# A two-layer transformer on one core: the feed-forward's turns counted on VectorE alone, its queues reordered, the identity inside the output weights

## The reference

```python
o = s @ w_o
return s + o                                  # end of the third step, s: heads' outputs

hidden = x @ W1 + b1                          # 128 -> 512
imag = w_imag * sin(theta + hidden * 0.1)
quantum_phase = cos(theta) * w_real + sin(theta) * w_imag
q = hidden + quantum_phase * imag * 0.1
out = relu(q) @ W2 + b2                       # 512 -> 128
x = x + out
```

## Time and profile before

| | us |
|---|---|
| three executions | 1871.88, 1875.59, 1877.41 (median 1875.59) |
| the profiled execution, its own time | 1856.86 |
| its span, first to last instruction | 1855.0 |
| mean granted TensorE clock, share of full speed | 0.943 |
| busy in the span: PE, DVE, ACT, POOL | 1708.5 (92%), 1372.3 (74%), 1143.6 (62%), 308.6 (17%) |
| chain that ended last: PE, DVE, ACT, issue, POOL, DMA | 73%, 14%, 4%, 4%, 3%, 3% |
| last instruction of the second attention ends | 1738.85 |
| last finish ends (its store follows) | 1852.33 |

### The profile page before, as it was taken

The page is one execution under the profiler, slowest core; times in us unless marked ns, Lnnn a source line. Parts: engine busy times, 40 slices in busy tenths (PEclk is TensorE's granted clock), DMA queues, the critical chain, the costliest instruction groups (busy, mean ns, idle before and its releaser), DMA issues.

```text
span 1855.0 us, 30812 instructions
## 1 busy us (share of the span) xinstructions
PE 1708.5 (92%) x10574; PEld 723.3 (39%) x10574; DVE 1372.3 (74%) x2373; ACT 1143.6 (62%) x2396; POOL 308.6 (17%) x407
## 2 busy tenths in 40 slices
PE   6599999999999899998789999999999999999876
PEld 3244444444443366655312232232222222322455
DVE  7678888788887155464897888888888888882486
ACT  4156666756664543333406777777777777777776
POOL 5000000002231237363500000000000000000265
PEclk9589999999998899999658999999999999998998
DMA  9555454423400012222411111111111111000000
GB/s 258 137 118 127 131 141 118 49 31 56 58 22 14 26 35 71 68 67 60 119 33 14 18 18 18 18 18 18 18 18 18 18 18 18 1 2 1 1 23 24
DMA packets 97577, 93.73 MB, mean 51 GB/s; under 512 B 47214, under 2 KB 75507, under 8 KB 95376
## 3 DMA queue, kind: packets, MB, share of 16 engines
q1 hardware_dynamic: 87360, 53.70, 16.7%
q0 software_dynamic: 9920, 37.87, 5.8%
q10 hardware_dynamic: 144, 0.20, 0.1%
HBM read 48.03 MB, written 40.86 MB: 48 GB/s over the span
## 4 chain that ended last, share of the span: by engine, by line
PE 73%; DVE 14%; ACT 4%; issue 4%; POOL 3%; DMA 3%; SPq 0%; POOLq 0%; DVEq 0%; ACTq 0%
PE ps L877 20%; PE ps L861 18%; PE ps L828 17%; DVE rowmax L1513 7%; PE ps L1038 2%; PE ps L1058 2%; PE ps L1030 2%; PE ps L1048 2%; PE ps L893 2%; PE ps L831 1%; PE ps L864 1%; ACT probs L1251 1%; DMA V<-v 1%; PE ps L1015 1%; DVE K L1857 1%
## 5 line engine op out<-in xcount | busy, mean ns | idle before, releaser
L1513 DVE TENSOR_REDUCE rowmax<-ps 128x1 f32<-128x1024 f32 (+7 forms) x1024 | 977.1, 987 | 220.4 <-PE ps L828 120.9
L1251 ACT ACTIVATE probs<-ps 128x512 f32<-128x512 f32 (+3 forms) x1280 | 604.0, 537 | 268.8 <-PE ps L864 128.7
L828 PE MATMUL ps<-K,Q 72*128 72x512 bf16 (+3 forms) x1792 | 535.6, 377 | 40.2 <-DVE rowmax L1513 18.1
L861 PE MATMUL ps<-Q,K 75*128 75x512 bf16 (+3 forms) x1792 | 559.7, 364 | 11.0 <-ACT probs L1251 6.4
L861 PEld LDWEIGHTS ps<-Q,K 75*128 75x128 bf16 x1792 | 168.5, 98 | 373.4 <-ACT probs L1251 128.6
L877 PE MATMUL ps<-probs,V 128*9 128x512 f32 (+3 forms) x2560 | 289.9, 543 | 0.0
L828 PEld LDWEIGHTS ps<-K,Q 72*128 72x128 bf16 x1792 | 159.4, 99 | 280.3 <-DVE rowmax L1513 88.4
L1251 ACT ACTIVATE wu<-ps 128x512 f32<-128x512 f32 x256 | 142.0, 608 | 44.7 <-PE ps L861 43.9
L1251 ACT ACTIVATE wg<-ps 128x512 f32<-128x512 f32 x256 | 143.7, 601 | 29.0 <-PE ps L861 27.1
L616 POOL TENSOR_SCALAR rtmp<-mv 128x4 f32<-128x4 f32 x8 | 1.9, 233 | 805.6 <-DVE mv L1429 805.6
L831 PE MATMUL ps<-causal,identb 128*128 128x128 bf16 x512 | 117.0, 230 | 0.0
(11 more groups left out here) (239 smaller groups left out, 1667.8 us busy)
## 6 DMA issues: line engine op xcount, KB each, us to landing
dispatch<-wg POOLq DMA_DIRECT2D x16, 1170.0 KB, 7.9
Q<-q_parts SPq DMA_DIRECT2D x288, 64.0 KB
K<-k_parts SPq DMA_DIRECT2D x144, 64.0 KB
Q<-dispatch SPq DMA_DIRECT2D x78, 65.0 KB, 1.8
q_parts<-Q POOLq DMA_DIRECT2D x12, 384.0 KB, 4.0
probs<-returned SPq DMA_DIRECT2D x8, 512.0 KB, 3.9
V<-v SPq DMA_DIRECT2D x16, 144.0 KB
K<-k_parts SPq DMA_DIRECT2D x144, 16.0 KB
```

The source lines that it names most:

```text
L828: last = pe.matmul(buf[:, c:e], Q[0:CROSS, slot, j, i * P:(i + 1) * P], K[0:CROSS, slot, kj, c:e], start=True, stop=not diag)
L861: last = pe.matmul(ps[:, bank, c:HALF], K[0:KROWS, q, kj, t * P:(t + 1) * P], Q[0:KROWS, q, j, h * HALF + c:(h + 1) * HALF], start=True, s ...
L1251: act.activation(prob(l, 4 * m + j)[:, c:HALF], ps[:, B_BANKS[(4 * m + j) % 3], c:HALF], ACT.Exp, scale=SCALE).then_inc(sl["exp_done"], 1)
L1513: dve.tensor_reduce(rowmax[:, par, 8 * j + i:8 * j + i + 1], score_a(i % 2)[:, 0:hd.keys(i)], AX, ALU.max).then_inc(sl["max_done"], 1)
```

## The change

- `turn_counts` on GpSimd goes. `reduced` on VectorE does the whole step with two instructions: `turns` = `arg` + ROUND, then (`turns` - ROUND) - `arg`, with a wait for the first between them. The result has the other sign, so the sine's scale is negative.
- The second reading of the hidden product by ScalarE (L1348, into `hid`) goes. `mixed` reads PSUM bank 2+c itself, and b1 comes in as the bias of relu. So `ff_hidden` waits for `mixed` of the group before, where it waited for `hid`.
- GpSimd adds the identity to `wo1` once, when the weights are there, ahead of the fills of the dispatch buffers. The products with the identity as moving side (L1100) go. For groups 2 to 7, TensorE adds x instead: identity times the tile of `x`, into the same sums. For the early groups 0 and 1 it does not, and VectorE adds `x` as before.
- For groups 2 to 7, VectorE takes the statistics from PSUM bank 1 and no longer adds to `x`; ScalarE copies the bank into `x` (`keep_x`). `add_b2`, the normalisation and the next product into that bank wait for that copy.
- The attention's output is turned where it lies; the copy into `tokens` (L1828) and its semaphore go.
- The order changes on three engines. VectorE: stage 2 of u+1 behind mixed(u-1,2), the statistics of u+2 behind mixed(u,0), finish(u-1) behind mixed(u,1). TensorE: the output product of (u-1,0) is no longer last in the call before but third in its own call; those of (u-1,1) and (u-1,2) follow hidden(u,2), and (u-1,3) ends the call. ScalarE: the copies into `hT_all` and `aT` come at the end of step c = 1, behind sine and relu; `keep_x` comes behind the argument of c = 3.

```diff
@@ -155,7 +155,7 @@
...
     "tensor": [{}, {1: (0, 0), 3: (0, 1), 6: (0, 2), 7: (1, 0), 9: (1, 1)}],
-    "vector": [{}, {0: (0, 0), 3: (0, 1), 5: (0, 2), 6: (1, 0), 9: (1, 1), 11: (1, 2)}],
+    "vector": [{}, {3: (0, 1), 5: (0, 2), 9: (1, 1), 11: (1, 2)}],
@@ -405,6 +405,7 @@
...
         rstd_first = sem("rstd_first")
+        wo1_whole = sem("wo1_whole")
@@ -427,8 +428,8 @@
...
         ff = {n: sem("ff_" + n) for n in
-              ("attn_staged", "a_turned", "a_ready", "wo_out", "added", "stats", "rstd", "normed", "turned", "h_ready",
-               "hidden", "arg", "hid", "turns", "reduced", "sine", "mixed", "relu", "y_out", "y_ready", "stored")}
+              ("a_turned", "a_ready", "wo_out", "x_kept", "added", "stats", "rstd", "normed", "turned", "h_ready",
+               "hidden", "arg", "reduced", "sine", "mixed", "relu", "y_out", "y_ready", "stored")}
@@ -693,6 +694,8 @@
...
             pool.wait_ge(w_in, 16 * len(weights))
+            own.done(pool.tensor_tensor(wo1[:, :], wo1[:, :], ident[:, :], ALU.add))
+            pool.sem_inc(wo1_whole, 1)
@@ -725,16 +728,10 @@
...
-            def turn_counts(u, c):
-
-                pool.wait_ge(ff["arg"], FC * u + c + 1 + AT_ONE)
-                apart(pool)
-                own.done(pool.tensor_scalar(turns[:, c, :], arg[:, c, :], 1.0, ROUND, ALU.mult, ALU.add))
-                pool.tensor_scalar(turns[:, c, :], turns[:, c, :], -ROUND, 1.0,
-                                   ALU.add, ALU.mult).then_inc(ff["turns"], 1)
-
...
                 pool.wait_ge(ff["stored"], 16 * u + AT_ONE)
+                if u >= 2:
+                    pool.wait_ge(ff["x_kept"], u - 1)
@@ -743,8 +740,6 @@
                 for c in range(FC):
-                    if now:
-                        turn_counts(u, c)
@@ -1087,18 +1082,23 @@
...
                 if stage == 0:
-                    pe.wait_ge(ff["attn_staged"], u + 1)
+                    pe.wait_ge(s[1]["attn_done"], 2 * 4 * (u // 2 + 1) + AT_ONE)
...
                         pe.wait_ge(ff["h_ready"], u)
-                    turn(tokens, first, ff["a_turned"])
+                    if u > 0:
+                        pe.wait_ge(ff["a_ready"], u)
+                    turn(attn[:, u * GT:(u + 1) * GT, :], first, ff["a_turned"])
...
                     pe.wait_ge(ff["a_ready"], u + 1)
-
+                    if not early:
+                        pe.wait_ge(ff["stats"], u)
+                        pe.wait_ge(ff["x_kept"], u - 2)
                     for k in range(GT):
-                        pe.matmul(ps[:, second, k * D:(k + 1) * D], aT[:, k * P:(k + 1) * P], wo1[:, :],
-                                  start=True, stop=False)
-                        last = pe.matmul(ps[:, second, k * D:(k + 1) * D], aT[:, k * P:(k + 1) * P], ident[:, :],
-                                         start=False, stop=True)
+                        last = pe.matmul(ps[:, second, k * D:(k + 1) * D], aT[:, k * P:(k + 1) * P], wo1[:, :],
+                                         start=True, stop=early)
+                        if not early:
+                            last = pe.matmul(ps[:, second, k * D:(k + 1) * D], ident[:, :], x[:, u * GT + k, :],
+                                             start=False, stop=True)
@@ -1108,7 +1108,7 @@
...
                 if not isinstance(u, int) or u > 0:
-                    pe.wait_ge(ff["hid"], FC * u + c + 1 - FC)
+                    pe.wait_ge(ff["mixed"], FC * u + c + 1 - FC)
@@ -1126,23 +1126,23 @@
...
                     ff_hidden(u, 1)
+                if before:
+                    ff_out(u - 1, 0)
...
                     ff_prepare(u + 2, 0)
+                if now:
+                    ff_hidden(u, 2)
...
                     ff_out(u - 1, 1)
-                if now:
-                    ff_hidden(u, 2)
+                    ff_out(u - 1, 2)
...
                 if before:
-                    ff_out(u - 1, 2)
                     ff_out(u - 1, 3)
-                if now:
-                    ff_out(u, 0)
@@ -1152,6 +1152,7 @@
...
             project(1)
+            pe.wait_ge(wo1_whole, 1)
@@ -1339,33 +1340,34 @@
...
+            def keep_x(u):
+
+                act.wait_ge(ff["stats"], u + 1)
+                act.activation(x[:, bass.ts(u, GT), :], ps[:, 1, :].rearrange("p (t d) -> p t d", t=GT), ACT.Copy)\
+                    .then_inc(ff["x_kept"], 1)
+
...
                                scale=0.1 / TWO_PI).then_inc(ff["arg"], 1)
-                act.activation(hid[:, c, :], ps[:, 2 + c, :], ACT.Identity, bias=b1c[:, c:c + 1])\
-                    .then_inc(ff["hid"], 1)
...
                 act.wait_ge(ff["reduced"], FC * u + c + 1)
-                act.activation(arg[:, c, :], arg[:, c, :], ACT.Sin, scale=2.0 * PI_IN).then_inc(ff["sine"], 1)
+                act.activation(arg[:, c, :], arg[:, c, :], ACT.Sin, scale=-2.0 * PI_IN).then_inc(ff["sine"], 1)
...
                 act.wait_ge(ff["y_out"], FC * u + c + 1)
-                act.activation(act1[:, c, :], arg[:, c, :], ACT.Relu).then_inc(ff["relu"], 1)
+                act.activation(act1[:, c, :], arg[:, c, :], ACT.Relu, bias=b1c[:, c:c + 1]).then_inc(ff["relu"], 1)
...
                         hidden(u, c)
-                    if c == 1 and following:
-                        ff_prepare(u + 1, 1)
-                    if c == 1 and more:
-                        ff_prepare(u + 2, 0)
-
+                    if c == 3 and more:
+                        keep_x(u + 2)
@@ -1374,6 +1376,10 @@
...
                         relu(u - 1, c + 2)
+                    if c == 1 and following:
+                        ff_prepare(u + 1, 1)
+                    if c == 1 and more:
+                        ff_prepare(u + 2, 0)
@@ -1822,19 +1828,27 @@
...
             def ff_prepare(u, stage, early=False):
-                second = 3 if early else 1
-                if stage == 0:
-                    dve.wait_ge(ff["a_turned"], u + AT_ONE)
-                    dve.tensor_copy(tokens[:, :, :], attn[:, bass.ts(u, GT), :]).then_inc(ff["attn_staged"], 1)
-                elif stage == 1:
+                if stage == 1 and early:
...
                     dve.wait_ge(ff["wo_out"], u + 1)
-                    own.done(dve.tensor_tensor(xs, xs, ps[:, second, :].rearrange("p (t d) -> p t d", t=GT), ALU.add))
+                    own.done(dve.tensor_tensor(xs, xs, ps[:, 3, :].rearrange("p (t d) -> p t d", t=GT), ALU.add))
                     statistics(u, ff["stats"])
+                elif stage == 1:
+                    dve.wait_ge(ff["wo_out"], u + 1)
+                    dve.wait_ge(ff["rstd"], u)
+                    for k in range(GT):
+                        last = dve.bn_stats(stats[:, k, :], ps[:, 1, k * D:(k + 1) * D])
+                    own.done(last)
+                    apart(dve)
+                    for k in range(GT):
+                        last = dve.bn_aggr(mv[:, k, :], stats[:, k, :])
+                    last.then_inc(ff["stats"], 1)
...
                         dve.wait_ge(ff["turned"], u)
+                    if u >= 2:
+                        dve.wait_ge(ff["x_kept"], u - 1)
@@ -1847,14 +1861,15 @@
...
-                dve.wait_ge(ff["turns"], FC * u + c + 1)
-                dve.tensor_tensor(arg[:, c, :], arg[:, c, :], turns[:, c, :], ALU.subtract)\
+                dve.wait_ge(ff["arg"], FC * u + c + 1 + AT_ONE)
+                own.done(dve.tensor_scalar(turns[:, c, :], arg[:, c, :], ROUND, None, ALU.add))
+                dve.scalar_tensor_tensor(arg[:, c, :], turns[:, c, :], ROUND, arg[:, c, :], ALU.subtract, ALU.subtract)\
...
                 a = arg[:, c, :]
-                dve.scalar_tensor_tensor(a, a, coef[:, c:c + 1], hid[:, c, :], ALU.mult, ALU.add)\
+                dve.scalar_tensor_tensor(a, a, coef[:, c:c + 1], ps[:, 2 + c, :], ALU.mult, ALU.add)\
@@ -1874,9 +1889,11 @@
...
                         mixed(u - 1, c + 2)
-                    if c != 1 and more:
-                        ff_prepare(u + 2, max(0, c - 1))
-                    if c == 2 and before:
+                    if c == 0 and before and following:
+                        ff_prepare(u + 1, 2)
+                    if c == 2 and more:
+                        ff_prepare(u + 2, 1)
+                    if c == 3 and before:
...
             feed_forward(0, before=False)
```

## The result

The changed kernel takes 1860.14 us (median of 12 runs, 1856.35 to 1869.66), the kernel before 1874.49 (12 runs, 1868.78 to 1883.62): a ratio of 0.9933 with an interval of 0.9915 to 0.9951, 14.4 us less.

What follows compares the result with a forecast made beforehand. It took VectorE, busiest but waiting on GpSimd's turns in a loop with ScalarE, as the bound. 1.75-0.7+3.5+8.9 = 13.45 us saved: 1843.4 for a profile, 1862.1 as median; own range 1857 to 1867, wider 1852 to 1871.

Steps and rivals of the forecast that it cites:

- Early products: Groups 0 and 1, under the last attention quad: dropping their identity products on TensorE saves 1.75 us.
- Start of the feed-forward: Up to group 2's normalisation: ScalarE copies hT and aT behind the first sine and its table load; 0.7 us lost.
- The ring: Steady period, normalisation to normalisation: TensorE's products 5.59 us, then VectorE's statistics to normalisation 6.72; 12.31 us without the b2 meeting.
- the reduction: VectorE's rounding addition, wait for its own semaphore and subtract-subtract, per chunk: 0.42+0.10+0.67 = 1.19 us.
- The meeting with the addition of b2: Steady periods: GpSimd's addition of b2 runs beside VectorE's normalisation, drawing it from 1.12 to 2.10 us; costs 1.0 us.
- rival A: Steady periods: the addition of b2 misses the normalisation and falls on the next reduction; period 12.3 us, total 1856; chance 0.18.
- the saving of 3.5 us in five periods: Five steady periods of the feed-forward: each falls from 14.01 to 13.3 us, 5x0.7 = 3.5 us saved.
- Rival C: Feed-forward: TensorE falls to its lower clock, which counts in full; period 18.2 us, total about 1898; chance 0.08.
- The tail: Group 7's normalisation to the last finish: 29.74 us falls to 20.4, plus 0.5 for lower clock; 8.9 us saved.
- the last link: End of the kernel: rest of the mix 0.08, relu 0.7, output product 1.1, rest of the finish; 2.0 us.
- B: VectorE's rounding addition takes 0.74 us, not 0.42; costs 5.8 us more, total 1868; chance 0.12.
- D: Steady period: the turns weren't what it waited for; it stays 14.0 us, only 1.75 us saved, total 1874; chance 0.07.

Runs made afterwards that it cites:

- experiment 3: Kernel before with only the turns moved from GpSimd to VectorE; old order, identity products and x as before: 1866.36 us, ratio 0.9984.
- experiment 7: Kernel before with turns on VectorE and the mix reading PSUM, without ScalarE's second reading of the hidden product: 1865.16 us, ratio 0.9963.
- experiment 1: Changed kernel with GpSimd's addition of b2 held back by one more wait, to run beside VectorE's statistics: 1852.79 us, ratio 0.9915.
- experiment 2: Changed kernel with the turns put back on GpSimd, all else kept: 1869.87 us, ratio 0.9989 to the kernel before.
- experiment 8: Changed kernel with the old order put back on VectorE, TensorE and ScalarE: 1859.32 us, ratio 0.9917 to the kernel before.
- experiment 5: Changed kernel with the wo1 product ahead of the two output products and aT copied ahead of the sine: 1851.09 us, ratio 0.9873.
- experiment 6: Changed kernel with the wo1 product first and the addition of b2 held back until that product is out: 1846.23 us, ratio 0.9858.

## Why the prediction was right, and where its terms were off

*Early products.* Priced at 1.75 us, measured 2x(1.89-0.99) = 1.80: right. But the stretch from the last row maximum to the last attention division became 4.6 us shorter. The other 2.8 lie ahead of these products, where both profiles of before ran TensorE at 0.59 and the kernel after at 1.00. All eight profiled versions with the change's early part took 57.4 to 57.6 us for the stretch. Experiments 3 and 7, which keep the early part of before, took 59.15 and 60.3, and experiment 3 ran it at 1.00 throughout: 1.7 more than after, the products alone. So the early part of before doesn't always bring the lower clock, and where it came, it set in before the first of the early products: at 1702.30 two instructions took 1.01 us (0.79 at the same place in after, from 1707.60), and the first early transposes ran at 1711.18. What sets it stays open; the prediction had no term for it. That the 2.8 us belong to the change is not shown.

*Start of the feed-forward.* Predicted 0.7 lost, measured 0.93. About half of it is one more meeting: an addition of b2 drew the subtract-subtract at 1762.70 out to 1.67 us, and experiment 1, where it meets nothing, starts in 14.15 us instead of 14.61.

*The ring.* It was the right ring. TensorE's part was 5.59, measured 5.62 (the normalisation's end at 1793.80 to the statistics at 1799.42). VectorE's part with the meeting was 7.72, measured 7.41 (1799.42 to 1806.83). The difference is the reduction: predicted 1.19, measured 1.04, twice. The wait between its two instructions, which I took at 0.10 from another pair, is 0.03 here (0.40 from 1772.96, next at 1773.39), and the step behind the second is 0.61, not 0.67. Without the meeting I had 12.31; experiment 1 shows 12.04.

*The meeting with the addition of b2.* Predicted 1.0 in each of five periods. It came in four, and experiment 1 took it away for 1.0. In the fifth the normalisation had 1.11, and the addition fell on the next reduction: rival A, for one period.

*The term that failed* is the saving of 3.5 us in five periods; it was 2.56. By the mended ring it should have been larger: 0.3 more in each period and 1.0 in the last. Rival C's mechanism, a lower clock that counts in full, fits what took it away: the granted clock was 0.88 in two of five periods, as before, and there, with TensorE in series on the ring, it cost 1.7 us in the second period (14.71 against 13.03) and 1.6 in the fifth (13.67 against experiment 1's 12.04, neither with a meeting), 3.3 in all, where it had cost 0.1. The prediction said that this clock now counts in full, and then put it in the ring's time nowhere but in C. C's full price (21 us, the whole feed-forward at half clock) did not come; the right use of the earlier trace rows was to charge two periods of five. On the rule named beside C (the Trainium skill, "TensorE: Matmul & The Clock Gate", HAM oscillation), that waits between bursts of products can throw the clock back again and again, the trace stands between: two periods of five show such a fall, three do not.

*The tail.* Predicted 20.4 and 0.5 for the lower clock, measured 20.19. The granted clock was 1.00 up to the last finish, so the 0.5 wasn't needed. VectorE is busy 17.6 of it and idle 2.6, most of that the 2.1 us ahead of the last finish. Its terms were off and nearly cancel: a reduction was 1.04, not 1.19, eight times over (1.2 less); the idle time is 2.6 where the last link was priced at 2.0; and the addition of b2 met two instructions, not one, 1.4 us in all where 1.0 was priced (they take 0.69 and 0.42 when quiet):
```profile
1833.92 1.67 DVE L1866 SCALAR_TENSOR_TENSOR K<-K 128x512 f32<-128x512 f32 x1
...
1843.87 0.86 DVE L1865 TENSOR_SCALAR K<-K 128x512 f32<-128x512 f32 x1
```
Experiments 2, 3, 7 and 8 show what the prediction didn't separate: the tail falls from 29.7 to about 25 with either part alone, turns on VectorE in the old order (25.3, 24.5 and 24.8 in experiments 3, 7 and 8) or the new order with turns on GpSimd (25.0), and to 20.2 only with both. The clock goes along with it and isn't separated: 0.83 in the tail of before, 0.81 in experiment 2's, 0.93 in those of 3, 7 and 8, 1.00 in after's.

*Rivals and rule.* B: the rounding addition took 0.43, not 0.74. D: experiment 2 speaks against it, for with the turns back the gain is gone. For the periods it was half right: with only the turns moved, experiment 3 shortened five periods by 0.3 us, and what it gained came from the tail. The rule of the Trainium skill, "VectorE: DVE Perf Modes", section on the TRN2 errata, that a PSUM source is dearer, is not borne out: the mix out of PSUM took 0.74 us and, where GpSimd is quiet, 0.75 out of SBUF, and four statistics from PSUM 0.89 us against 0.87.

*Sum.* By the profiles 11.2 and 4.6 make 15.8; the medians differ by 14.4; the prediction had 13.45. Two errors offset each other: a clock that cost 3.3 us in the ring, and one that gave 2.8 back ahead of it. That the total came within 1 us of the medians' difference is in part luck. Read in a row, the profiles show where the feed-forward's 11.2 us came from: 113.48 before, 108.49 with the turns on VectorE (experiment 3), 104.46 with the mix out of PSUM as well (7), 102.72 with all but the new order (8), 102.30 after. Of the 18.7 us between the first profile and the median, which no row explained, 12 are what the second profile has more ahead of the last attention quad.

## What to carry to other kernels

When work moves off a helper engine, the chain that is left runs through engines that had slack. Walk that ring in full, and charge it with everything that was hidden before, a lower clock in some periods among it. An addition that waits for a store lands where the store's time puts it: tie it to a point where its neighbour doesn't suffer, which here shortened the feed-forward by 7.7 us in the profile for one wait (about 3 us by the ratios). And try the parts of a new order alone: the whole of this one left the feed-forward where it was (102.72 to 102.30), two of its moves alone brought it to 88.36.

## What the runs showed of the hardware that wasn't expected

- Beside GpSimd only those VectorE instructions were drawn out whose operands all lay in SBUF: the subtraction 1002 ns, the normalisation 2.14 us against 1.11. The mix with an operand in PSUM kept 738 ns, and statistics out of PSUM 0.89 us, all but the first 0.1 of it beside the addition of b2.
- The granted clock fell in kernels whose TensorE waited longer for the normalisation: up to 2.8 us in experiment 2 (0.81 to 0.90 in four periods of five), 2.36 in after (two), 1.9 in experiment 5 (four), and not at 1.33 or 0.9 (experiments 1 and 6). Where that wait was shortened, the lower clock went with it. It is no rule: TensorE in experiment 3 waited up to 2.5 us for a copy of VectorE's, and one period of five fell. Only the kernel before has two profiles (the same two periods fell in both), so how far this repeats from one execution to the next is not shown for the others.
- Two executions of one kernel differed by 12 us in the stages ahead of the last attention quad, and by 0.02 at most in every period of the feed-forward.
